# Scores and maxima of an attention layer from stacked keys and queries, in place of row-tiled matmuls

## The chip, the cores and the metric

The kernel runs on one core of a Trainium2 chip. The metric is the time of the whole kernel on the device in microseconds, lower is better. Engines are named TensorE (PE; PEld is its weight load), VectorE (DVE), ScalarE (ACT), GpSimd (POOL) and SyncE (SP, which here only issues DMAs).

## The reference

The input x is 4 batches of 1024 tokens of 512 features, float32. Three layers follow one another, each on the normalised x and each added to it: a feed-forward layer with ternary weights (half its result is added), an attention layer, and the same feed-forward layer again.

```python
x = x + 0.5 * ffn(layernorm(x))
kqv = layernorm(x) @ Wqkv + bqkv                      # 16 heads of 32
scores = einsum('bsnh,btnh->bnst', k, q) / sqrt(32)   # k: rows, q: columns
scores = triu(scores) - 10000 * tril(ones, k=-1)
attn = softmax(scores, axis=2)
x = x + einsum('bnkq,bknh->bqnh', attn, v) @ Wo + bo
x = x + 0.5 * ffn(layernorm(x))
```

A matmul of the attention layer gets float32 accuracy from three faster ones: each operand is held as a high part and the rest (HI and LO), and HI·HI, LO·HI and HI·LO are summed in the bank.

## The kernel before

The work is cut into slots. Each batch has 40 of them, ten rows for each of 4 groups of 4 heads; 21 slots come before (the head) and 10 after (the tail). Every engine walks through the same slots in order, and what a slot holds is written out by hand in tables of rows (GROUP0_ROWS and so on, from L86): `P` is a projection of keys or queries (12 matmuls of 128x512 at L1173), `A` a block of maxima, `M`, `N` and `C` the rows of the maxima, the rows of the inverses and the end of a chunk, `V` the values, `O` the output projection, `T1` to `T3` transposes of normalised tiles, `F1` and `F2` the feed-forward products, `X` loads of x, `LV` and `LO` loads of weights, `W` the preparation of a weight. Ahead of its uses each slot has one step of scores, and the values of the step before it.

A step of scores (`scores`, L1253) works on 4 heads, each in a bank of its own. The 32 rows of keys and queries of a head lie on partitions 32h to 32h+31, so that the matmuls of the four heads use different rows of the array: three terms of four matmuls of 32 rows (L1266), then four of 2 rows (L1274) that add minus the maximum of each query, from `mneg`. ScalarE exponentiates the four banks into `prob` (L1099), GpSimd masks the diagonal ones (L808), and the next slot's TensorE multiplies them with the values (L1294, 128 rows to 32 columns, float32).

The maxima come from a second pass over the scores, in the other orientation: block `A` (L1232) makes 3 terms of four 32-row matmuls into four banks. VectorE masks each bank, writes it to `masked_scores` and keeps its maximum (`maximum`, L900); ScalarE takes the exponentials of that with their sum (`block_sums`, L1065), the first three heads in the slot of the block and the fourth in the next slot, after that slot's exponentials. TensorE transposes the maxima of a chunk (`M`), ScalarE and VectorE split them into `mrow`, and SP copies them to `mneg` (`rows`, L660). Seven banks are a ring in order of use; the eighth gathers the values.

A projection is split by ScalarE (high half with the bias, `high`, L1019) and VectorE (low half, `low`, L881), straight into `kT` and `qT`, where scores and maxima read it. Per group there are four: keys and queries of chunk 0 and of chunk 1. SP's queue is in the order of the slots (L692 and behind): stores, kept weights, loads, rows of the maxima and inverses, and the weights of the next group behind the second pair of projections (`load_qk`, L649).

```python
for term, (x, y) in enumerate(((HI, HI), (LO, HI), (HI, LO))):
    for kb, off, at in parts:
        for h in range(4):
            row = slice(HD * h, HD * h + HD)
            nc.tensor.matmul(psum(u, h)[:, at:at + CW - off],
                             kT[g % 2][row, x, P * kb:P * kb + P], query_piece(b, g, c)[row, y, off:CW], ...)
```

Of the kernel before, what the change touches and what calls it, by code (L numbers as in the profile page):

```python
# [5 lines left out]
F32 = mybir.dt.float32  # L6
# [6 lines left out]
P = 128  # L13
# [5 lines left out]
CW = 512  # L19
# [55 lines left out]
def pieces(b, g):  # L75
    second = (Q_, K_) if g == 0 else (K_, Q_)
    return [("P", b, g, K_, 0), ("P", b, g, Q_, 0)] + [("P", b, g, j, 1) for j in second]
# [9 lines left out]
    "C P | A | LO",  # L87
# [7 lines left out]
    "T3.2 F2.1 | A | X3.5",  # L95
    "F2.2 P | A",
)
GROUP1_ROWS = (
    "C T3.3 P | A | X3.6",
# [7 lines left out]
    "T3.6 F2.5 | A | LV X1.1",  # L107
# [3 lines left out]
    "C T1.0 F2.7 P | A | X1.3",  # L111
# [5 lines left out]
    "M T1.6 F1.5 | A",  # L117
    "T2.2 T1.7 F1.6 | A",
    "T2.3 F1.7 | A",
    "T2.4 P | A",  # L120
)
GROUP3_ROWS = (
    "C T2.5 P | A",
    "N M T2.6 V.0 | A",
    "T2.7 V.1 | A",
    "C P | A",
    "P | A",
    "N V.2 | A",
    "M V.3 V.4 | A",
    "V.5 | A",  # L130
    "V.6 V.7 | A",
    "P | A",
# [3 lines left out]
    "V.4 | A | X1.0",  # L136
    "N M V.5 | A | X1.1 | W",
# [6 lines left out]
    "F1.1 | A",  # L144
# [3 lines left out]
    "C F1.2 P | A",  # L148
# [7 lines left out]
    "F1.5 | A",  # L156
# [3 lines left out]
    "C P | A",  # L160
# [7 lines left out]
    "T2.6 T2.7 | A",  # L168
    "P | A",
)  # L170
FIRST_GROUP3_ROWS = (
    "C P | A",
    "N M V.0 | A",
    "V.1 | A",
    "C P | A",
    "P | A",
    "N V.2 | A",
    "M V.3 V.4 | A",
    "V.5 | A",
    "V.6 V.7 | A",  # L180
    "P | A",
# [3 lines left out]
    "C P | A | LO",  # L185
# [7 lines left out]
    "F2.1 | A",  # L193
# [3 lines left out]
    "C P | A | X3.5",  # L197
    "N M T3.2 P | A",
# [6 lines left out]
    "T3.5 O.7 | A",  # L205
# [3 lines left out]
    "C P | A",  # L209
# [54 lines left out]
    "P | A | | W",  # L264
# [88 lines left out]
for s in SLOTS:  # L353
    small = [u not in PRODUCTS for u in s.uses()]
    assert small == sorted(small, reverse=True)
SETUP_USES = 6
# [11 lines left out]
class Banks:  # L368


    def __init__(self):
# [12 lines left out]
        def use(u):  # L384
            nonlocal full, freed
            take(u, 4 if u[0] == "A" else 1)
            if u != BIAS:
                full += 1
                self.full[u] = full
# [16 lines left out]
def macaron_kernel(nc, x, wqkv, bqkv, wo, bo, wf, bf, out):  # L406
    with ExitStack() as ctx:
# [24 lines left out]
        ones = sb("ones", [P, P])  # L432
        onesr = sb("onesr", [P, P], F32R)
        pick = sb("pick", [8, P], F32R)
# [14 lines left out]
        mrow = sb("mrow", [4 * QPC, 2, 2, P], F32R)  # L449
        rrow = sb("rrow", [4 * QPC, 2, P], F32R)  # L450
# [7 lines left out]
        hi_done = sem("hi_done")  # L458
# [877 lines left out]
```

## Time and profile before

| | |
|---|---|
| median of 3 runs | 1118.87 us (1113.22, 1118.87, 1119.31) |
| profiled execution: own time, span | 1115.44 us, 1113.7 us |
| mean granted clock of TensorE | 0.983 of full speed |
| TensorE busy, matmuls | 1067.9 us (96%), 9472 |
| ScalarE, VectorE, GpSimd busy | 921.7 (83%), 738.9 (66%), 344.0 us (31%) |
| DMA | 77.71 MB, 20.5% of 16 engines on the SP queue |

The span is the time between the first and the last instruction of the profiled execution; its own time has the start and the end around it. Matmuls overlap, so their mean duration is longer than the distance from one to the next: what a use of TensorE costs is read from the start of its first matmul to the start of the next use.

### The profile page before, as it was taken

The page shows a single profiled execution, that of the slowest core. Times are in us where ns is not written, and L with a number is a line of the kernel's source. Part 1 is how long each engine was busy: PE and PEld are TensorE (multiplying, and loading weights), DVE is VectorE, ACT ScalarE, POOL GpSimd, SP SyncE. Part 2 cuts the span into 40 slices and gives each one's busy share as a digit, 9 for nine tenths or more (in the row PEclk, how much of TensorE's full clock was granted, in tenths as well). Part 3 has the DMA queues.
Part 4 walks back from the last instruction along what each step waited for, and adds up shares of the span by engine and source line. Part 5 has one row for each costly group of instructions (what it writes and reads, how often), then busy time and mean ns, then how long its engine had stood idle before and what let it go on. Part 6 is the DMA issues. An engine that isn't in the chain of part 4 may idle for free.

```text
span 1113.7 us, 26124 instructions
## 1 busy us (share of the span) xinstructions
PE 1067.9 (96%) x9472; PEld 691.1 (62%) x9472; DVE 738.9 (66%) x2306; ACT 921.7 (83%) x2577; POOL 344.0 (31%) x471
## 2 busy tenths in 40 slices
PE   5799999999999999999999999999999999999896
PEld 3576656565666565665666666675666666665465
DVE  6866577787535767789644766789744667765344
ACT  2269998999989989889988988878988998999641
POOL 3841232233001313345201322435401322311343
PEclk8898999999999999999999999999999999998999
DMA  6463211021004110421112211421112212000121
GB/s 207 153 217 125 97 50 40 3 78 50 24 19 154 32 59 31 158 73 43 38 41 87 77 59 50 144 78 40 51 40 86 69 40 69 21 12 13 60 66 38
DMA packets 42015, 77.71 MB, mean 70 GB/s; under 512 B 5536, under 2 KB 11680, under 8 KB 41888
## 3 DMA queue, kind: packets, MB, share of 16 engines
q1 hardware_dynamic: 41888, 76.04, 20.5%
q8 instruction: 76, 1.25, 0.5%
q14 instruction: 51, 0.42, 0.1%
HBM read 49.81 MB, written 25.17 MB: 67 GB/s over the span
## 4 chain that ended last, share of the span: by engine, by line
PE 76%; ACT 11%; DVE 6%; issue 2%; POOL 2%; DMA 1%; SPq 0%; DVEq 0%; ACTq 0%; POOLq 0%
PE bank L1173 31%; PE bank L1294 10%; PE bank L1232 10%; PE bank L1266 10%; PE bank L1195 7%; ACT masked_scores L1073 6%; ACT prob L1099 4%; PE bank L1184 3%; PE bank L1274 3%; DVE masked_scores L909 2%; DVE st L859 1%; DMA xt<-in_L_attn_x_dram 1%; DVE hn L878 1%; POOL xt L769 1%; PE bank L1251 1%
## 5 line engine op out<-in xcount | busy, mean ns | idle before, releaser
L909 DVE CUSTOM_DVE_ANT_0 masked_scores<-bank,mask 128x512 f32<-128x512 f32 (+3 forms) x768 | 379.6, 554 | 221.3 <-PE bank L1232 220.2
L1073 ACT ACTIVATE masked_scores<-masked_scores,mst 128x512 f32<-128x512 f32 (+3 forms) x768 | 467.7, 620 | 2.9 <-DVE mst L909 2.9
L1099 ACT ACTIVATE prob<-bank 128x512 f32<-128x512 f32 (+1 forms) x640 | 302.0, 559 | 58.5 <-PE bank L1274 57.4
L1173 PE MATMUL bank<-hT,wqk 128*128 128x512 f32 x768 | 190.9, 397 | 0.0
L808 POOL TENSOR_SCALAR_AFFINE_SELECT prob<-prob 128x512 f32<-128x512 f32 (+1 forms) x96 | 78.6, 819 | 346.5 <-ACT prob L1099 345.8
L1266 PE MATMUL bank<-qT,kT 32*128 32x512 f32 (+2 forms) x2304 | 169.6, 378 | 4.5 <-DVE kT L886 1.6
L1232 PEld LDWEIGHTS bank<-kT,qT 32*128 32x128 f32 x2304 | 94.4, 185 | 115.6 <-issue 52.8
L1232 PE MATMUL bank<-kT,qT 32*128 32x512 f32 (+2 forms) x2304 | 161.2, 377 | 3.4 <-ACT prob L1099 2.6
L1173 PEld LDWEIGHTS bank<-hT,wqk 128*128 128x128 f32 x768 | 140.4, 188 | 37.9 <-ACT prob L1099 8.2
L1073 ACT ACTIVATION_READ_ACCUMULATOR masked_scores<-masked_scores,mst 128x1 f32 x768 | 156.4, 204 | 0.0
L1266 PEld LDWEIGHTS bank<-qT,kT 32*128 32x128 f32 x2304 | 97.7, 185 | 70.4 <-issue 48.4
L1195 PE MATMUL bank<-wfT,hts 128*128 128x512 f32 x512 | 138.3, 414 | 1.5 <-DVE hts L884 1.5
L1294 PE MATMUL bank<-prob,v 128*32 128x512 f32 (+3 forms) x1344 | 138.7, 500 | 0.0
L1195 PEld LDWEIGHTS bank<-wfT,hts 128*128 128x128 f32 x512 | 94.4, 194 | 24.5 <-ACT prob L1099 2.6
L769 POOL TENSOR_TENSOR xt<-xt,hb 128x512 f32<-128x512 f32 x64 | 82.3, 1286 | 77.0 <-DVE hn L878 77.0
L1173 PE MATMUL bank<-wvo,hts 128*128 128x512 f32 x384 | 97.2, 403 | 5.0 <-POOL hts L776 5.0
L1173 PE MATMUL bank<-wvo,hT 128*128 128x512 f32 x384 | 96.1, 402 | 1.2 <-DVE qT L886 1.2
L1173 PEld LDWEIGHTS bank<-wvo,hts 128*128 128x128 f32 x384 | 70.7, 190 | 24.4 <-ACT prob L1099 6.0
L1173 PEld LDWEIGHTS bank<-wvo,hT 128*128 128x128 f32 x384 | 71.3, 191 | 19.5 <-ACT prob L1099 2.7
L1184 PE MATMUL bank<-ident,hn 128*128 128x128 f32 x384 | 59.7, 284 | 13.5 <-DVE hn L878 13.5
L1274 PE MATMUL bank<-mneg,onesr 2*128 2x512 f32 (+2 forms) x768 | 69.9, 350 | 2.1 <-DMA mneg<-mrow 2.1
L859 DVE BATCH_NORM_STATS2 st<-xt 128x6 f32<-128x512 f32 x96 | 65.9, 686 | 5.2 <-DMA xt<-in_L_attn_x_dram 3.2
(87 smaller groups left out, 971.7 us busy)
## 6 DMA issues: line engine op xcount, KB each, us to landing
wqk<-weight_scratch SPq DMA_DIRECT2D x30, 512.0 KB, 3.4
wvo<-weight_scratch SPq DMA_DIRECT2D x20, 512.0 KB, 6.0
xt<-in_L_attn_x_dram SPq DMA_DIRECT2D x32, 256.0 KB, 4.2
residual_scratch<-xt SPq DMA_DIRECT2D x32, 256.0 KB, 2.0
xt<-residual_scratch SPq DMA_DIRECT2D x32, 256.0 KB, 3.1
out_dram<-xt SPq DMA_DIRECT2D x32, 256.0 KB, 2.0
o<-in_L_attn_Wqkv_dram SPq DMA_DIRECT2D x12, 256.0 KB, 4.7
weight_scratch<-o SPq DMA_DIRECT2D x6, 512.0 KB, 3.0
```

The lines of the kernel that those rows point to most:

```text
L769: nc.gpsimd.tensor_tensor(to, to, (bo2 if l == 1 else hb)[:, :], ALU.add).then_inc(xb_done[l], 1)
L808: nc.gpsimd.affine_select(out=part, in_=part, compare_op=ALU.is_ge, fill=0.0, base=0, pattern=[[0, 4], [0, m], [1, P]], channel_multiplier ...
L909: nc.vector.tensor_tensor_reduce(masked_scores[:, h, at:at + n], psum(u, h)[:, at:at + n], mask[:, off:off + n], -SCALE, BIG, ALU.add, ALU ...
L1073: nc.scalar.activation(of, of, ACT.Exp, bias=mst[:, c + kc, to:to + 1], scale=-1.0, accum_out=ssum[:, c + kc, to:to + 1]).then_inc(a_free, 1)
L1099: nc.scalar.activation(prob[:, at % 2, h, off:CW], psum(("S", b, n), h)[:, off:CW], ACT.Exp, scale=SCALE)\
L1173: m = nc.tensor.matmul(psum(u), left(x, k), right(y, k), start=(n == 0), stop=(n == len(terms) - 1))
L1184: m = nc.tensor.transpose(psum(u)[:, P * k:P * k + P], hn[:, TURN[u] % 2, P * k:P * k + P], ident[:, :])
L1195: m = nc.tensor.matmul(psum(u), h[:, part, k, :], wfT[:, k, :], start=(k == 0 and part == HI), stop=(k == KC - 1 and part == LO))
L1232: m = nc.tensor.matmul(psum(u, h)[:, at:at + n], query_piece(b, g, c)[row, x, P * r:P * r + P], kT[g % 2][row, y, CW * kc:CW * kc + n], st ...
L1266: nc.tensor.matmul(psum(u, h)[:, at:at + CW - off], kT[g % 2][row, x, P * kb:P * kb + P], query_piece(b, g, c)[row, y, off:CW], start=(ter ...
L1274: m = nc.tensor.matmul(psum(u, h)[:, at:at + CW - off], onesr[row, :], mneg[row, c, off:CW], start=False, stop=(kb == keys[-1]))
L1294: m = nc.tensor.matmul(accv[HD * h:HD * h + HD, off:CW], v_of(b, g, kb, h), prob[:, at % 2, h, of:of + CW - off], start=(kb == 0), stop=(k ...
```

## The change

Keys and queries of a projection are now stacked. `kst` holds for each head, on partitions 0 to 95, the keys' parts HI, LO, HI, and on 96 and 97 ones; `qst` holds HI, HI, LO of the queries, and on 96 and 97 the high and low part of minus the maximum. One matmul a head over 98 rows gives the scores, one over 96 rows the block of maxima. To bring the four heads of a projection, which come out on 128 partitions, onto 32 partitions side by side, the columns of the weights are reordered so that head h of feature q is on partition 4q + h; the projection is split into one tile, `stage`, and three DMAs of 256 KB from it build a stack (`stack`, on SP, in the slots that MOVES gives). ScalarE waits with the next high half until the last stack has landed. Each head of scores and maxima has its own bank wait and its own signal.

Beside that: three stacks each of keys and queries; `prob` is a ring of 6 heads (8 before), `masked_scores` 2 (4 before), `mrow` one buffer (2 before); ScalarE's order is exponentials of heads 0 and 1, the fourth sum of the last block, exponentials of heads 2 and 3; the mask of a diagonal step is cut in two where the ring ends; and the rows are rearranged: projections stand in rows 8, 9, 1 and 2 of a group (8, 9, 2 and 4 for group 0 of a batch that follows, before 9, 0, 1, 2 or 9, 0, 3, 4), and none in row 0.

```diff
 def pieces(b, g):
-    second = (Q_, K_) if g == 0 else (K_, Q_)
-    return [("P", b, g, K_, 0), ("P", b, g, Q_, 0)] + [("P", b, g, j, 1) for j in second]
+    return [("P", b, g, K_, 0), ("P", b, g, Q_, 0), ("P", b, g, Q_, 1), ("P", b, g, K_, 1)]
...
 GROUP0_ROWS = (
-    "C P | A | LO",
+    "C | A | LO",
     "N M P | A | X3.0",
     "P | A | X3.1",
...
-    "T3.2 F2.1 | A | X3.5",
-    "F2.2 P | A",
+    "F2.1 P | A | X3.5",
+    "T3.2 P | A",
...
+NPIECE, NPROB = 3, 6
+STACK, ROWS = 3 * HD, 3 * HD + 2
...
+MOVES = [[] for _ in SLOTS]
+for at, s in enumerate(SLOTS):
+    for u in s.uses():
+        if u[0] == "P":
+            old = outlived(u)
+            MOVES[at + 1 if old is None else max(at + 1, SLOT_OF[old])].append(u)
...
-        kT = [sb(f"kT{n}", [P, 2, S], F32R) for n in range(2)]
-        qT = sb("qT", [P, 3, 2, CW], F32R)
-        mneg = sb("mneg", [P, CHUNKS, CW], F32R)
-        prob = sb("prob", [P, 2, 4, CW])
+
+        kst = [sb(f"kst{n}", [P, 4, CW], F32R) for n in range(NPIECE)]
+        qst = [sb(f"qst{n}", [P, 4, CW], F32R) for n in range(NPIECE)]
+        stage = sb("stage", [P, 2, CW], F32R)
+        prob = sb("prob", [P, NPROB, CW])
...
-        masked_scores = sb("masked_scores", [P, 4, CW])
-        rall = sb("rall", [8, CW], F32R)
+        masked_scores = sb("masked_scores", [P, 2, CW])
...
+        def heads_inside(w, of):
+
+            return of.rearrange("p (k h q) -> p k q h", k=KC, h=4) if w[0] == "QK" else of
...
+            def stack(u):
+
+                sp.wait_ge(ring_free, freed(u))
+                if outlived(u) is not None:
+                    sp.wait_ge(s_full, 4 * outlived(u) + 4)
+                n, _ = piece(u)
+                to, parts = (kst[n], (HI, LO, HI)) if u[3] == K_ else (qst[n], (HI, HI, LO))
+                for j, part in enumerate(parts):
+                    sp.dma_start(to[HD * j:HD * j + HD, :, :].bitcast(F32), stage[:, part, :].bitcast(F32))\
+                        .then_inc((kst_in if u[3] == K_ else qst_in)[n], 16)
...
+            for n in range(NPIECE):
+                nc.gpsimd.memset(kst[n][STACK:ROWS, :, :].bitcast(F32), 1.0).then_inc(set_pool, 1)
...
                 for h in range(4):
-                    if EARLIER[u] is not None:
-                        dve.wait_ge(a_free, block_at(EARLIER[u], h))
+                    dve.wait_ge(ring_full, full(u) - 3 + h)
+                    if h >= 2:
+                        dve.wait_ge(a_free, block_at(u, h - 2))
+                    elif EARLIER[u] is not None:
+                        dve.wait_ge(a_free, block_at(EARLIER[u], h + 2))
...
                 if kind == "P":
...
+                    at = PROJECTIONS.index(u)
+                    if at:
+                        act.wait_ge(*stacked(PROJECTIONS[at - 1]))
+                    i = nc.scalar.activation(stage[:, HI, :], psum(u), ACT.Identity, bias=bias_of(u[3], u[2]))
...
-                    exponentials(b, s.step)
+                    exponentials(b, s.step, (0, 1))
                 if k and SLOTS[k - 1].blocks:
                     block_sums(SLOTS[k - 1].blocks[-1], (3,))
+                if s.step is not None:
+                    exponentials(b, s.step, (2, 3))
...
                 elif kind == "A":
                     _, b, g, c, kc, _ = u
...
+                    pe.wait_ge(*stacked(("P", b, g, Q_, c)))
+                    pe.wait_ge(*stacked(("P", b, g, K_, kc)))
+                    for h in range(4):
+                        bank_free(u, h)
                         for j, r, at, keys, _ in block_tiles(u):
                             n = max(HALF, keys)
...
+                            m = nc.tensor.matmul(psum(u, h)[:, at:at + n], queries_of(b, g, c)[0:STACK, h, P * r:P * r + P],
+                                                 keys_of(b, g, kc)[0:STACK, h, 0:n], start=(j == 0), stop=(j == len(u[5]) - 1))
+                        m.then_inc(ring_full, 1)
...
                 if keys[0] == 0:
                     pe.wait_ge(mrow_in[c], 32 * group(b, g))
...
+                for h in range(4):
+                    bank_free(u, h)
+                    for kb, off, at in parts:
+                        key = P * (kb % QPC)
+                        m = nc.tensor.matmul(psum(u, h)[:, at:at + CW - off], keys_of(b, g, kb // QPC)[0:ROWS, h, key:key + P],
+                                             queries_of(b, g, c)[0:ROWS, h, off:CW], start=(kb == keys[0]), stop=(kb == keys[-1]))
+                    m.then_inc(s_full, 1)
```

## Rows read from the trace of the kernel before

**Rows 1.** The page: busy time by engine, and the chain that ended last.
```profile
PE 1067.9 (96%) x9472; PEld 691.1 (62%) x9472; DVE 738.9 (66%) x2306; ACT 921.7 (83%) x2577; POOL 344.0 (31%) x471
...
PE 76%; ACT 11%; DVE 6%; issue 2%; POOL 2%; DMA 1%; SPq 0%; DVEq 0%; ACTq 0%; POOLq 0%
...
PE bank L1173 31%; PE bank L1294 10%; PE bank L1232 10%; PE bank L1266 10%; PE bank L1195 7%; ACT masked_scores L1073 6%; ACT prob L1099 4%; PE bank L1184 3%; PE bank L1274 3%; DVE masked_scores L909 2%; DVE st L859 1%; DMA xt<-in_L_attn_x_dram 1%; DVE hn L878 1%; POOL xt L769 1%; PE bank L1251 1%
```

**Rows 2.** Busy time in stretches: PE, PEld, DVE, ACT, POOL (instructions), clock, DMA share, GB/s.
```profile
500.00:525.00 25.00, 23.80 (x212) 14.43 (x210) 24.42 (x71) 21.83 (x56) 13.80 (x20) 1.00 0.13 44
...
550.00:575.00 25.00, 25.00 (x209) 15.41 (x208) 13.09 (x41) 23.21 (x60) 0.00 (x0) 1.00 0.13 44
...
66.00:72.00 6.00, 6.00 (x50) 4.76 (x49) 4.04 (x19) 3.24 (x10) 4.45 (x4) 1.00 0.93 290
```

**Rows 3.** Timeline of TensorE, batch 2: start us, length us, instructions merged.
```profile
612.04 3.04 PE L1173 MATMUL bank<-hT,wqk 128*128 128x512 f32 x12
...
615.01 0.97 PE L1266 MATMUL bank<-qT,kT 32*128 32x512 f32 x12
...
615.80 0.42 PE L1274 MATMUL bank<-mneg,onesr 2*128 2x512 f32 x4
...
616.15 0.86 PE L1294 MATMUL bank<-prob,v 128*32 128x256 f32 x16
...
621.01 0.98 PE L1266 MATMUL bank<-qT,kT 32*128 32x512 f32 x12
...
622.16 1.07 PE L1294 MATMUL bank<-prob,v 128*32 128x512 f32 x8
...
623.15 0.97 PE L1232 MATMUL bank<-kT,qT 32*128 32x512 f32 x12
...
624.05 1.20 PE L1173 MATMUL bank<-wvo,hts 128*128 128x512 f32 x4
```

**Rows 4.** Timeline of TensorE where full-size products meet other uses.
```profile
586.17 5.73 PE L1173 MATMUL bank<-wvo,hT 128*128 128x512 f32 x24
...
1063.82 2.09 PE L1195 MATMUL bank<-wfT,hts 128*128 128x512 f32 x8
...
1065.75 2.89 PE L1173 MATMUL bank<-wvo,hts 128*128 128x512 f32 x12
...
1075.24 2.09 PE L1195 MATMUL bank<-wfT,hts 128*128 128x512 f32 x8
...
1077.27 0.86 PE L1294 MATMUL bank<-prob,vx 128*32 128x256 f32 x16
```

**Rows 5.** Timeline of the SP queue in row 2 of a group.
```profile
610.41 1.12 SPq L664 DMA_DIRECT2D mneg<-mrow  x2
...
611.63 0.38 SPq L657 DMA_DIRECT2D wqk<-weight_scratch  x1
```

**Rows 6.** Timeline of ScalarE and of VectorE around the same row.
```profile
608.79 0.19 ACT L1073 ACTIVATION_READ_ACCUMULATOR masked_scores<-masked_scores,mst 128x1 f32 x1
...
615.44 0.69 ACT L1025 ACTIVATE qT<-bank,bqk 128x512 fp32r<-128x512 f32 x1
...
608.85 0.27 DVE L886 SCALAR_TENSOR_TENSOR mrow<-bank,mrow 16x128 fp32r<-16x128 f32 x1
...
616.16 0.75 DVE L886 SCALAR_TENSOR_TENSOR qT<-bank,bqk,qT 128x512 fp32r<-128x512 f32 x1 [1.99 <-ACT qT L1025]
```

**Rows 7.** The page: DMA issues, KB of each and median us to landing.
```profile
wqk<-weight_scratch SPq DMA_DIRECT2D x30, 512.0 KB, 3.4
...
residual_scratch<-xt SPq DMA_DIRECT2D x32, 256.0 KB, 2.0
```

**Rows 8.** Timelines of TensorE and ScalarE in the head.
```profile
60.72 3.02 PE L1173 MATMUL bank<-hT,wqk 128*128 128x512 f32 x12
...
68.28 0.98 PE L1232 MATMUL bank<-kT,qT 32*128 32x256 f32 x24
...
63.77 0.69 ACT L1025 ACTIVATE qT<-bank,bqk 128x512 fp32r<-128x512 f32 x1 [1.52 <-PE bank L1173]
```

More of the change, by code:

```diff
@@ L155 @@
     "T1.5 | A",
-    "F1.5 | A",
+    "F1.5 P | A",
     "P | A",
@@ L196 @@
 LAST_GROUP1_ROWS = (
-    "C P | A | X3.5",
-    "N M T3.2 P | A",
+    "C T3.2 | A | X3.5",
+    "N M P | A",
     "F2.2 P | A | X3.6",
@@ L355, with piece, outlived @@
     assert small == sorted(small, reverse=True)
+PROJECTIONS = [u for u in USES if u[0] == "P"]
+NPIECE, NPROB = 3, 6
+STACK, ROWS = 3 * HD, 3 * HD + 2
+def piece(u):
+    n = 2 * (u[1] * GROUPS + u[2]) + u[4]
+    return n % NPIECE, n // NPIECE + 1
+def outlived(u):
+    n = 2 * (u[1] * GROUPS + u[2]) + u[4] - NPIECE
+    if n < 0:
+        return None
+    last = (6, 9) if u[3] == K_ else (2, 9)
+    return n // 2 * STEPS + last[n % 2]
+SLOT_OF = {s.b * NSTEP + s.step: k for k, s in enumerate(SLOTS) if s.step is not None}
+MOVES = [[] for _ in SLOTS]
[4 more added lines that the diff above has]
+            MOVES[at + 1 if old is None else max(at + 1, SLOT_OF[old])].append(u)
+assert [u for moves in MOVES for u in moves] == PROJECTIONS
 SETUP_USES = 6
@@ L387, in use @@
             if u != BIAS:
-                full += 1
+                full += 4 if u[0] == "A" else 1
                 self.full[u] = full
@@ L458, in macaron_kernel @@
         hi_done = sem("hi_done")
+        kst_in, qst_in = ([sem(f"kst_in{n}") for n in range(NPIECE)], [sem(f"qst_in{n}") for n in range(NPIECE)])
         s_full, s_exp = sem("s_full"), sem("s_exp")
@@ L549, in before, with keys_of, queries_of, stacked @@
             return (b, g - 1) if g else (b - 1, GROUPS - 1)
-        def query_piece(b, g, c):
-            return qT[:, (group(b, g) * CHUNKS + c) % 3, :, :]
+        def keys_of(b, g, kc):
+            return kst[piece(("P", b, g, K_, kc))[0]]
+        def queries_of(b, g, c):
+            return qst[piece(("P", b, g, Q_, c))[0]]
+        def stacked(u):
+            n, times = piece(u)
+            return (kst_in if u[3] == K_ else qst_in)[n], 48 * times
+        def place(n, h):
+            return (4 * n + h) % NPROB
+        def head_runs(n):
+            m = min(4, NPROB - place(n, 0))
+            return [(0, m)] + ([(m, 4 - m)] if m < 4 else [])
         def chunk(b, n):
@@ L707, in _ @@
                         store(u)
+                for u in MOVES[k]:
+                    stack(u)
                 for n in SLOTS[k - 1].weights if k else []:
@@ L1093, in high_output, with exponentials @@
                 i.then_inc(o_hi, 1)
-            def exponentials(b, n):
+            def exponentials(b, n, heads):
                 off = live(n % STEPS)
                 at = step(b, n)
-                for h in range(4):
-                    nc.scalar.activation(prob[:, at % 2, h, off:CW], psum(("S", b, n), h)[:, off:CW], ACT.Exp, scale=SCALE)\
+                for h in heads:
+                    act.wait_ge(s_full, 4 * at + h + 1)
+                    if 4 * at + h >= NPROB:
+                        act.wait_ge(value_done, (4 * at + h - NPROB) // 4 + 1)
+                    nc.scalar.activation(prob[:, place(at, h), off:CW], psum(("S", b, n), h)[:, off:CW], ACT.Exp, scale=SCALE)\
                         .then_inc(s_exp, 1)
```

172 lines of the change are left out of this document (74 added, 98 removed).

## The prediction

> **What bounds the kernel now.** Read the page first: TensorE is busy 96% of the span, ScalarE 83%, VectorE 66%, and the chain that ended last lies on TensorE for 76% [rows 1]. Its costliest members are the twelve-matmul products of L1173 (31%); scores (L1266 and L1274, 13%) and maxima (L1232, 10%) come next. So the question is what TensorE pays for scores and maxima. Then the busy time by stretch: between 550 and 575 us TensorE has no gap and ScalarE has 1.8 us left of 25; between 500 and 525, where transposes are dense, VectorE is the fullest at 24.4 and TensorE is short by 1.2 [rows 2]. Whatever ScalarE is made to wait for has little room. Then TensorE's timeline, a slot at a time: from 615.01 to 621.01, 6.0 us [rows 3]. Last, the SP queue and ScalarE in row 2 of a group, since the change puts a transfer between two of ScalarE's steps there.
>
> **Scores and maxima on TensorE.** A full block of scores now costs 1.14 us (615.01 to 616.15): three rounds of four concurrent 32-row matmuls to 615.80, then one round of 2-row ones. A full block of maxima costs 0.90 (623.15 to 624.05): three rounds [rows 3]. The change makes each four matmuls, one a head, with 98 or 96 rows. Their price is that of a product's matmul: 24 take 5.73 us and 12 take 3.04, so each further one takes (5.73 - 3.04)/12 = 0.224, call it 0.227, in the middle of the reading [rows 3, 4]. Four make 0.91. What lies between two uses: eight matmuls (1.82) and the next full-size product starts at 1.93, a gap of 0.11; before values it is 2.03, a gap of 0.21 [rows 4]; twelve (2.72) before scores as they are now take 612.04 to 615.01, 2.97, a gap of about 0.22 once a late wait of 0.03 is taken off [rows 3].
> So scores become 0.91 + 0.21 = 1.12, less by 0.02. Maxima become 0.91 + 0.11 = 1.02, more by 0.12: they lose a round, since three terms that ran four heads at a time become four full-width streams. The step from a product to scores falls from 0.22 to 0.11, less by 0.11. Values keep their 0.99 [rows 3]. Net: -0.01 a slot, over 160 slots **-2 us**. 3840 of the 9472 matmuls go, but hardly any streaming time. Both ends: if full-size uses follow each other with no gap, each slot saves another 0.22 (-37 us in all); if every head's matmul, which now has its own bank wait before it, pays the 0.11, six more a slot are +0.66, or +106 us. I take the value in between, since waits that are already met don't show inside the products.
> The Trainium skill (TensorEngine Tiling (Array Packing), Tiling Modes) says that a change of tiling mode drains TensorE. The change takes two of four such changes out of a slot; by that rule alone scores and maxima should be a gain, and the sum would be that of the first rival below. The rows agree that a change costs something (0.21 against 0.11), but it is small beside the lost round.
>
> **The stack.** Each of the 64 projections now goes to one staging tile, and three transfers of 256 KB copy it. ScalarE may not write the next projection's high half before the last stack has landed. Landing: one store of 256 KB takes 2.0 us from issue, one load of 512 KB 3.4 [rows 7]; at 290 GB/s, the most that a stretch shows at a DMA share of 0.93 [rows 2], 768 KB take 2.7 us, and with about 1.1 of fixed time 3.8. Bounds: 2.0, if the three run side by side, and 10.2, three times the 512 KB load. I take 3.8.
> - Rows 1 and 2 of a group hold the second pair. In row 2 SP is busy with the rows of the maxima until 611.53 and then with a weights' load [rows 5]. These wait for the low half of the maxima's rows, which VectorE begins at 608.85, right behind its last maximum. With two score buffers instead of four that maximum waits for ScalarE's sum of the second head, whose read now begins at 608.79 [rows 6]; a maximum is then still to be made, so all of this comes about 0.7 us later. The stack is thus issued at about 612.8 and, behind the 512 KB load, lands near 617.5. ScalarE wants the stage at 615.44 [rows 6]: a stall of about 2 us, and behind ScalarE stand the next exponentials, behind VectorE's low half the bank that the next maxima need. TensorE is ahead by part of it; I take 1.2 us for each of the 12 groups that have this pair: **+14**. Bounds 0 and 3 us each, 0 to 36.
> - Rows 8 and 9 hold the first pair. No other rows are queued on SP, the stack is issued about 2.2 us after the slot begins and lands at 6.0, when ScalarE wants it (0.4 us after TensorE ends a slot of about 6 us, as at 615.44): 0.2 for 15 groups, **+3**.
> - The first maxima of the next group are in row 1 and wait for the query stack of row 9, a full chain later: 0.7 high half, 0.75 low half [rows 6], 3.8 landing. With a full row 0 in between this is covered; where row 0 holds almost nothing (four groups) TensorE waits 1.5: **+6**.
> - In the head the second projection begins at 60.72, as the first ends, the maxima begin at 68.28 and ScalarE takes the query's high half at 63.77 [rows 8]; the DMA engines are 93% busy from 66 to 72 [rows 2]. Two stacks in a chain, each after a high and a low half and slowed to about 5 us (62 to 67, then 68.5 to 74), move the first maxima from 68.3 to about 74; two later pairs add some: **+9**, between 3 and 20.
>
> **The other edits.** Two score buffers: in rows with two transposes VectorE waits inside the maxima for sums that ScalarE does after two high halves; where VectorE is the last [rows 2], it is ahead of nothing and loses about 0.3 in some ten slots, **+3**. Semaphores by head: exponentials can begin after one matmul instead of sixteen, maxima after one instead of twelve, some 0.6 to 0.8 us earlier; where TensorE bounds, that is only latency, where it stood short of full it gives back some, **-6**. The ring of six for the exponentials, the split of the mask, the single row buffer, five small loads of biases, strided splits of the weights and three memsets of two rows: nothing each, hidden under the next slot's work or under the wait for the first weights; if that cover is gone, 0.3 to 2 us each. The wait for the maxima's rows moves ahead of all scores of steps 0 and 3: the rows' transfer ends well before, except in the last batch.
>
> **The sum.** The profiled execution took 1115.44 us, for a span of 1113.7, and stands 3.4 under the median of 1118.87. 1115.4 - 2 + 14 + 3 + 6 + 9 + 3 - 6 = **1142.4 us**, some 2% over either. What a measurement of this kernel can tell from no change is about 0.5%.
>
> **Rivals.**
> First, *faster*: the gaps between full-size uses vanish and the stacks land in 2 to 3 us, so only the head's cost and a part of the others is left: 1115 - 37 - 6 + 9 + 8 = 1089. For it speaks that the projections keep their slots' distance; against it, SP's two pairs of row transfers in front of the stack [rows 5]. 0.19.
> Second, *no change*: as forecast, but ScalarE's stalls are taken up by its slack of 1.8 us in 25 [rows 2] and the head's by idle engines: within 1113 to 1124. 0.13.
> Third, *much slower*: TensorE can't load a head's weights past that head's own bank wait. Place: every head of scores and maxima; price: 0.11 each, six more a slot, full or half: 1142 + 53 to 106, 1195 to 1248. It decides as soon as waits are met only just in time, which the two-buffer scheme makes likelier; against it, the sixteen matmuls of scores have four such waits now and show none of it. 0.16.
> The Trainium skill (TensorE: Matmul & The Clock Gate, Part 3) has it that each semaphore increment at a matmul's end is written one after another, 26.3 ns each; an estimate by that page for six more increments a slot is 25 us, which would make the sum 1167, in the same direction. No row here shows increments so close together.
>
> **How the numbers follow.** The forecast has 0.52, the rivals 0.19, 0.13 and 0.16. The range 1098 to 1188 holds the forecast with its bounds, the second rival and the upper part of the first; it leaves out the third and the fastest of the first. Faster by over 0.5%: 0.19; within: 0.13; slower: 0.68.
>
> **What would show it.** In the changed profile: 768 matmuls each for scores and maxima at a spacing near 0.227; from first maximum to next use 1.02; ScalarE's high halves of projections waiting for the stack's DMA, longest in row 2 of a group, some 1 to 2 us; TensorE's longest new wait at the first maxima in the head. The forecast is wrong if ScalarE never waits there, if a slot without projection falls below 5.8 us where it is 6.0 now, or if idle time shows between the heads' matmuls.

## The result, and the profile after

The changed kernel takes 1367.5 us (median of 4 runs, 1362.9 to 1372.3), the kernel before in the same runs 1116.2 (4 runs, 1113.2 to 1119.3): a ratio of 1.225, with a 95% interval of 1.219 to 1.231. It is slower by 251 us where 26 were forecast, and far outside the range of 1098 to 1188. One run in all is left out of the ratios: one of the four of **tiny** below, 1667.4 us at a granted clock of 0.56.

The page of the changed kernel: the lines that answer to [rows 1] and [rows 7], and the three groups of instructions that matter. Behind the bar of a group stand its busy time, the mean ns of one instruction, and the idle time before them with what ended most of it:

```profile
span 1365.8 us, 19813 instructions
...
PE 1152.2 (84%) x5632; PEld 776.5 (57%) x5632; DVE 762.6 (56%) x2306; ACT 949.7 (70%) x2577; POOL 356.1 (26%) x505
...
PE 46%; DMA 24%; ACT 9%; DVE 9%; SPq 6%; issue 3%; POOL 2%; DVEq 0%; ACTq 0%; POOLq 0%
...
L989 DVE CUSTOM_DVE_ANT_0 masked_scores<-bank,mask 128x512 f32<-128x512 f32 (+3 forms) x768 | 408.2, 556 | 329.9 <-ACT masked_scores L1153 225.4
...
L1310 PE MATMUL bank<-kst,qst 96*128 96x512 f32 (+2 forms) x768 | 220.2, 408 | 156.8 <-DVE stage L964 103.7
...
L1103 ACT ACTIVATE stage<-bank,bqk 128x512 fp32r<-128x512 f32 x64 | 43.9, 687 | 185.3 <-DMA qst<-stage 74.4
...
kst<-stage SPq DMA_DIRECT2D x96, 256.0 KB, 5.6
qst<-stage SPq DMA_DIRECT2D x96, 256.0 KB, 5.9
wqk<-weight_scratch SPq DMA_DIRECT2D x30, 512.0 KB, 4.7
```

DMA now holds 24% of the chain that ended last, where it held 1% [rows 1]. TensorE's idle time is 1365.8 - 1152.2 = 213.6 us against 1113.7 - 1067.9 = 45.8 before: 168 more. The other 84 of the 252 us are in its busy time, 1152.2 against 1067.9, though the changed slots take no longer when they run undisturbed (below): the granted clock averages 0.893 instead of 0.983. Behind the first 20 us of the trace, every idle stretch of TensorE of over 2.5 us lies in microseconds at a granted clock of 0.50, the lower of its two levels (1.2 GHz), or is followed by them; TensorE is busy for 233 us at that clock, where it was for 35 before.

Two new waits stand out. ScalarE's high halves of projections (L1103) waited 185 us, 148 of them for the stacks' DMA (the waits give 74.4 in 13 times for `qst` and 73.2 in 16 for `kst`), and VectorE's maxima (L989) waited 225 us for ScalarE's sums. The timelines of the four engines around row 2 of a group (start us, length us; row 2 begins at 449.05, row 3 at 454.48) show how the first reaches TensorE. In brackets stands how long the engine sat idle before, and what ended that:

```profile
451.38 1.98 SPq L736 DMA_DIRECT2D qst<-stage  x3
...
459.92 0.69 ACT L1103 ACTIVATE stage<-bank,bqk 128x512 fp32r<-128x512 f32 x1 [5.02 <-DMA qst<-stage]
...
460.64 0.75 DVE L964 SCALAR_TENSOR_TENSOR stage<-bank,bqk,stage 128x512 fp32r<-128x512 f32 x1 [5.89 <-ACT stage L1103]
...
456.29 0.73 PE L1310 MATMUL bank<-kst,qst 96*128 96x512 f32 x2
461.44 0.92 PE L1310 MATMUL bank<-kst,qst 96*128 96x512 f32 x2 [4.42 <-DVE stage L964]
462.30 0.79 PE L1328 MATMUL bank<-rows_of,pick 8*128 8x512 f32 x1
463.02 5.49 PE L1255 MATMUL bank<-wvo,hts 128*128 128x512 f32 x12
468.31 1.24 PE L1343 MATMUL bank<-qst,kst 98*128 98x512 f32 x4
```

The stack is issued from 451.38 and ScalarE goes on at 459.92, 8.5 us later. VectorE's low half stands behind ScalarE, and behind VectorE the bank of the third head of the maxima: TensorE stops for 4.42 us, and its next twelve matmuls then take 468.31 - 463.02 = 5.3 us, for which [rows 3] have 3.0. Row 3 lasts 13.8 us; in the kernel before the same row of the same group took 6.0.

The same happens at the other pair of projections, in rows 8 and 9. The stack of row 8 is issued in row 9 and still on its way when ScalarE wants the stage in row 0 of the next group:

```profile
424.65 1.93 SPq L736 DMA_DIRECT2D kst<-stage  x3
...
432.78 0.69 ACT L1103 ACTIVATE stage<-bank,bqk 128x512 fp32r<-128x512 f32 x1 [4.51 <-DMA kst<-stage]
...
434.31 1.07 PE L1310 MATMUL bank<-kst,qst 96*128 96x512 f32 x2 [3.45 <-DVE stage L964]
```

Over the whole trace ScalarE's wait for the stage costs TensorE 56 us in 12 rows 3 and 43 us in 14 rows 0; the maxima's own wait for a query stack adds 20.5 us in 12 rows 1 and 17.6 in the head.

The stack before that of row 2 is issued from 434.28. The busy time in stretches from then on (columns as in [rows 2]: length; PE, PEld, DVE, ACT and POOL busy; clock, DMA share, GB/s):

```profile
438.00:440.00 2.00, 1.55 (x8) 0.00 (x0) 1.93 (x9) 1.92 (x5) 0.00 (x0) 0.50 1.04 124
440.00:442.00 2.00, 0.00 (x0) 0.00 (x0) 0.01 (x1) 1.23 (x5) 0.68 (x1) 0.50 1.05 132
442.00:444.00 2.00, 1.63 (x7) 1.63 (x8) 0.80 (x7) 0.00 (x0) 0.00 (x0) 0.50 1.06 389
```

The DMA engines are full in all three, but bring 124 to 132 GB/s while the stack is copied and 389 when the four loads of `wvo` behind it run. That became the theory to test: **A, landing**, a transfer that writes 32 partitions is slow. Against it stood **B, structure**: the two score buffers, the single stage and the moved rows. Measured over the 64 stacks in the trace's landing records, from the first issue to the last packet of the third transfer, a stack takes a median of 8.1 us (7.8 to 9.8).

### The profile page after: what moved, and what is told of

It is laid out like the page before. It is cut to its first block, busy times and chain, and to the rows that moved or that the text cites. A ratio compares the mean times of both kernels' runs of the same rounds, so it can differ in the third digit from the quotient of the medians.

```text
span 1365.8 us, 19813 instructions
## 1 busy us (share of the span) xinstructions
PE 1152.2 (84%) x5632; PEld 776.5 (57%) x5632; DVE 762.6 (56%) x2306; ACT 949.7 (70%) x2577; POOL 356.1 (26%) x505
## 4 chain that ended last, share of the span: by engine, by line
PE 46%; DMA 24%; ACT 9%; DVE 9%; SPq 6%; issue 3%; POOL 2%; DVEq 0%; ACTq 0%; POOLq 0%
PE bank L1255 18%; DMA qst<-stage 15%; PE bank L1310 9%; DMA kst<-stage 8%; PE bank L1363 5%; PE bank L1277 5%; PE bank L1343 5%; SPq L736 4%; ACT masked_scores L1153 4%; DVE stage L964 3%; ACT stage L1103 2%; PE bank L1266 2%; DVE masked_scores L989 2%; ACT prob L1182 1%; SPq L745 1%
## 5 line engine op out<-in xcount | busy, mean ns | idle before, releaser
L989 DVE CUSTOM_DVE_ANT_0 masked_scores<-bank,mask 128x512 f32<-128x512 f32 (+3 forms) x768 | 408.2, 556 | 329.9 <-ACT masked_scores L1153 225.4
L1310 PE MATMUL bank<-kst,qst 96*128 96x512 f32 (+2 forms) x768 | 220.2, 408 | 156.8 <-DVE stage L964 103.7
L1182 ACT ACTIVATE prob<-bank 128x512 f32<-128x512 f32 (+1 forms) x640 | 318.6, 553 | 37.6 <-PE bank L1343 29.7
L1310 PEld LDWEIGHTS bank<-kst,qst 96*128 96x128 f32 x768 | 127.0, 207 | 295.4 <-DVE stage L964 115.9
L1343 PE MATMUL bank<-qst,kst 98*128 98x512 f32 (+2 forms) x768 | 189.9, 370 | 14.3 <-DVE mst L989 8.8
L885 POOL TENSOR_SCALAR_AFFINE_SELECT prob<-prob 128x512 f32<-128x512 f32 (+2 forms) x128 | 83.7, 658 | 423.0 <-ACT prob L1182 422.8
L1103 ACT ACTIVATE stage<-bank,bqk 128x512 fp32r<-128x512 f32 x64 | 43.9, 687 | 185.3 <-DMA qst<-stage 74.4
L1343 PEld LDWEIGHTS bank<-qst,kst 98*128 98x128 f32 x768 | 136.5, 199 | 52.9 <-DVE mst L989 20.8
L1277 PE MATMUL bank<-wfT,hts 128*128 128x512 f32 x512 | 153.2, 448 | 5.1 <-DVE hts L962 2.1
L964 DVE SCALAR_TENSOR_TENSOR stage<-bank,bqk,stage 128x512 fp32r<-128x512 f32 x64 | 48.0, 750 | 194.1 <-ACT stage L1103 194.1
```

The lines of the kernel that those rows point to most:

```text
L885: i = nc.gpsimd.affine_select(out=part, in_=part, compare_op=ALU.is_ge, fill=0.0, base=0, pattern=[[0, heads], [0, m], [1, P]], channel_mu ...
L964: i = nc.vector.scalar_tensor_tensor(dst, src, first[0], hi.bitcast(F32), first[1], ALU.subtract)
L989: nc.vector.tensor_tensor_reduce(masked_scores[:, h % 2, at:at + n], psum(u, h)[:, at:at + n], mask[:, off:off + n], -SCALE, BIG, ALU.add, ...
L1182: nc.scalar.activation(prob[:, place(at, h), off:CW], psum(("S", b, n), h)[:, off:CW], ACT.Exp, scale=SCALE)\
L1277: m = nc.tensor.matmul(psum(u), h[:, part, k, :], wfT[:, k, :], start=(k == 0 and part == HI), stop=(k == KC - 1 and part == LO))
L1310: m = nc.tensor.matmul(psum(u, h)[:, at:at + n], queries_of(b, g, c)[0:STACK, h, P * r:P * r + P], keys_of(b, g, kc)[0:STACK, h, 0:n], sta ...
```

## The experiments

Each run is compared with the kernel before on the same chip (1117 to 1118 us there). The diffs show the deciding lines, shortened and without bitcasts. In **tiny**, **spread**, **one** and the runs that leave stacks unfilled, the stacks are filled with ones at the start, and SP waits for that before its first slot.

### How much is the landing

**tiny**: each transfer of a stack brings 16 of 512 columns; all waits stay. The scores and maxima are computed mostly from the ones.

```diff
-    sp.dma_start(to[HD * j:HD * j + HD, :, :], stage[:, part, :])
+    sp.dma_start(to[HD * j:HD * j + HD, :, 0:16], stage[:, part, 0:16])
```

> Each of the three transfers of a stack copies 16 of the 512 columns, so 8 KB in place of 256 KB; waits, order and TensorE's work stay (the stacks hold mostly ones, so the output is another; both sets of stacks are filled once at the start). Theory A, the landing: the 252 us lost come from the time in which 768 KB land (8.5 us from the first issue in row 2 of a group, where ScalarE and then TensorE wait), and from the clock behind these waits. Then the time falls to 1105 to 1150, the granted clock is back at 0.97 or more, and ScalarE no longer waits for a stack by more than 10 us in all. Theory B, the structure: the waits come from the single stage, the two score buffers and the ring of banks by head, whatever the transfer carries. Then it stays above 1250, and idle time before the maxima stays above 80 us.

Measured: 1180.3 us, ratio 1.055 (1.053 to 1.058); a stack is complete after 3.1 us, the clock is at 0.965. 187 of the 251 us go with the bytes, so A carries most of it, and B, which allowed nothing below 1250, falls as the whole cause. But 62 us are left, more than A allowed, and ScalarE still waits 12.7 us for stacks where A had 10.

**spread**: all bytes, each transfer to 128 partitions of 2 KB in place of 32 of 8 KB. Scores and maxima are again not the reference's.

```diff
-    sp.dma_start(to[HD * j:HD * j + HD, :, :], stage[:, part, :])
+    sp.dma_start(to[:, j, :], stage[:, part, :])
```

> The same three transfers with all their 768 KB, but each writes one tile of 128 partitions by 2 KB in place of 32 partitions by four times 2 KB (values of the stacks are wrong so, which costs no time). Theory A1, the shape: the landing is slow because each transfer writes only 32 partitions (from 436 to 442 us the sixteen engines were full at 124 to 132 GB/s, and at 316 to 389 GB/s in the loads behind). Then a transfer lands in 3 to 4 us in place of 5.7, ScalarE's stall in row 2 shrinks to 0 to 2 us, and the time is 1130 to 1200. Theory A2, the bytes: 768 KB from SBUF to SBUF are slow in any shape; then landing and time stay within 2% of the changed kernel's 1367.

Measured: 1211.0 us, ratio 1.083 (1.081 to 1.086), 11 above the range of A1, which had nothing for the structure; A2 falls. The page's landings:

```profile
kst<-stage SPq DMA_DIRECT2D x96, 256.0 KB, 2.5
qst<-stage SPq DMA_DIRECT2D x96, 256.0 KB, 2.8
```

A transfer lands in 2.5 to 2.8 us instead of 5.6 to 5.9, a whole stack in 3.8 instead of 8.1. The same bytes, issued and waited for at the same places, cost 157 us less by their shape alone. ScalarE's waits for the stage in rows 3 fall from 69.6 to 29.4 us, those in rows 0 from 60 to nearly nothing.

**one**: only the first of the three transfers, and only it waited for; two thirds of a stack are left out.

```diff
-    for j, part in enumerate(parts):
+    for j, part in list(enumerate(parts))[:1]:
```

> Only the first of the three transfers is made, 256 KB to 32 partitions, and its 16 are waited for (two thirds of each stack keep ones). By A1, 256 KB at 130 GB/s take 2.0 us and some 2 us of fixed time: landing 4 us after the issue, 1130 to 1190. By theory B 1250 or more. If the cost goes by the number of bytes it should lie at a third of the way from the kernel with small transfers to the changed one, if it goes by a threshold (what ScalarE can be made to wait before TensorE feels it) nearer to the former.

Measured: 1218.0 us in a single run, above A1's range as well. A single transfer to 32 partitions is there after 4.0 us, and it costs about what three to 128 partitions cost in 3.8. The times follow when the stack is complete, not its bytes: 3.1, 3.8, 4.0 and 8.1 us go with 1180, 1211, 1218 and 1367, and 24, 768, 256 and 768 KB.

**traffic32**: the kernel before, with three copies of 256 KB to 32 partitions behind each projection that only later copies wait for.

```diff
+    for j in range(3):
+        sp.dma_start(scr[HD * j:HD * j + HD, :, :], hb[:, :]).then_inc(scr_in, 16)
```

> The kernel before, with the stack's traffic added and nobody waiting for it but the queue itself: behind each projection three transfers of 256 KB from one tile of 128 partitions to 32 partitions of a spare tile. If the traffic itself costs (loads and rows that it delays), the time is 1140 to 1200; if the cost is only in the waits for it, 1115 to 1125.

Measured: 1149.0 us, ratio 1.027 (1.025 to 1.029). The copies land in 5.9 us at the median, three of them in 8.1, with no stack in sight; the 512 KB loads of `wqk` land in 7.0 instead of 3.4 [rows 7]. Of the 31 us, 25 lie in six waits of TensorE for transfers that stood behind copies on the queue (five for the rows of the maxima, 16.0 us, one for a load of `wqk`, 9.3); the kernel before has one of these, 2.1 us. In the changed kernel TensorE waits once for rows of the maxima, 3.0 us, and never for such a load. So these 31 us are a cost of their own in this order of the queue and no part that can be taken off the 251: there, what A costs is the waiting for the stacks.

### Which partitions make a transfer slow

**shapes**: the kernel before, with two such copies behind each projection, in four shapes that take turns.

```diff
+    kind = (at + at // 4) % 4
+    for j in range(2):
+        if kind == 0:   sp.dma_start(scr[HD * j:HD * j + HD, 0:4, :], hb[:, :])      # L679
+        elif kind == 1: sp.dma_start(scr[0:64, 2 * j:2 * j + 2, :], hb[:, :])        # L681
+        elif kind == 2: sp.dma_start(scr[32:96, 2 * j:2 * j + 2, :], hb[:, :])       # L683
+        else:           sp.dma_start(scr[:, j, :], hb[:, :])                         # L685
```

> The kernel before, with two copies of 256 KB behind each projection that nobody but the next copies wait for, in four shapes that take turns: to 32 partitions x 8 KB, to partitions 0-63 x 4 KB, to partitions 32-95 x 4 KB, to 128 partitions x 2 KB. It is read by the landing of each shape and the DMA rate of its stretches. Theory A1 (the time is set by how many partitions are written): 32 partitions about 5.7 us as in the stacks, 64 about half way (4), both placements alike, 128 about 2.5. Theory A3 (the Trainium skill, SBUF - State Buffer, Door 1: partitions 0-31 and 32-63 share their ports, 64-95 have others): 0-63 lands as 32 does (about 5.7), 32-95 as 128 does (about 2.5 to 3). Theory A4 (a copy inside the core is slow in any shape): all four about 5.7; spread has already spoken against it. Whole time 1122 to 1150.

The view of each of the four lines (issue time ns, then the landings):

```profile
L679 SPq DMA_DIRECT2D scr<-hb x32: 594/604/1493, 63.9 to 985.4; - x32
...
DMA to landing us min/median/max: 4.2/5.4/7.9
...
L681 SPq DMA_DIRECT2D scr<-hb x32: 553/596/1027, 70.5 to 992.0; - x32
...
DMA to landing us min/median/max: 4.2/5.3/6.7
...
L683 SPq DMA_DIRECT2D scr<-hb x32: 571/603/624, 80.7 to 998.0; - x32
...
DMA to landing us min/median/max: 2.9/3.4/8.8
...
L685 SPq DMA_DIRECT2D scr<-hb x32: 497/560/603, 86.1 to 979.1; - x32
...
DMA to landing us min/median/max: 2.3/2.5/4.1
```

The two copies of a projection are issued one behind the other, so these are times under that load (the single copy of **one** took 4.0). 64 partitions from 0 on land hardly sooner (5.3) than 32 do (5.4), where A1 had 4; 64 from 32 on land in 3.4, 128 in 2.5. The two shapes of 64 differ in nothing but their place: it is not how many partitions, but which. The Trainium skill (SBUF — State Buffer, Door 1: The DMA port swizzle) says that partitions p and p + 32 share a port and that p + 64 has another, so that 0 to 63 reach no more ports than 0 to 31, half of all. The trace agrees that 0 to 63 gain next to nothing over 32. Two things differ. By the page 32 to 95 reach every port as 0 to 127 do, and A3 had them at 2.5 to 3; they need 3.4, for which no run gives the reason. And the rate falls further than the page's half, to 124 to 132 GB/s in the changed kernel where the loads have 384 to 389. The whole kernel takes 1117.3 us in a single run, against 1118.3: two copies that nothing waits for, mostly in faster shapes, cost nothing here.

**twoq**: the kernel after, complete, with the third transfer of a stack (to partitions 64 to 95) issued by GpSimd.

```diff
+    for u in MOVES[k]:        # GpSimd, ahead of its other work in a slot
+        pool.wait_ge(ring_free, freed(u)); pool.wait_ge(s_full, 4 * outlived(u) + 4)
+        pool.dma_start(to[HD * 2:HD * 3, :, :], stage[:, part, :]).then_inc(kst3_in[n] or qst3_in[n], 16)
```

> The kernel after with the third transfer of each stack (to partitions 64-95, whose ports are others than those of 0-63 by the rows of shapes) issued by GpSimd from its own queue while SP issues the first two; nothing is left out. Theory Q1 (two queues run side by side, so the stack is complete some 2 us earlier): 1280 to 1330 against 1367. Theory Q2 (the same engines serve both queues in turn; the Trainium skill, SBUF - State Buffer, Can I just issue two DMAs to hit both halves?, says they serialize): 1350 to 1390, the last part of a stack landing 8 us or more after the first issue as now.

Measured: 1367.9 us, ratio 1.224 (1.220 to 1.228), as the kernel after. The page's landings:

```profile
kst<-stage SPq DMA_DIRECT2D x64, 256.0 KB, 6.3
qst<-stage SPq DMA_DIRECT2D x64, 256.0 KB, 7.2
...
kst<-stage POOLq DMA_DIRECT2D x32, 256.0 KB, 6.1
qst<-stage POOLq DMA_DIRECT2D x32, 256.0 KB, 6.6
```

GpSimd issues its transfer 0.3 us after SP's first at the median, so they do run together. Each gets slower, and the stack is complete after 8.1 us as before. A second queue is no way out; this was Q2.

### What the structure costs

**before_ms2**: the kernel before with two score buffers, nothing else.

```diff
-    if EARLIER[u] is not None: dve.wait_ge(a_free, block_at(EARLIER[u], h))
+    if h >= 2: dve.wait_ge(a_free, block_at(u, h - 2))
+    elif EARLIER[u] is not None: dve.wait_ge(a_free, block_at(EARLIER[u], h + 2))
-    masked_scores[:, h, ...]
+    masked_scores[:, h % 2, ...]      # at both places, and the tile is [P, 2, CW]
```

> The kernel before, with two score buffers in place of four and the waits that go with it, nothing else. Theory B1 (the rest of the cost, 62 us with the stacks' bytes all but gone, comes from the coupling of VectorE's third maximum to ScalarE's first sum): 1150 to 1180. Theory B2 (it comes from the order of the rows, the projections moved) and theory B3 (it comes from the one stage, each projection waiting for the copy of the last, or from the heads' own waits): 1117 to 1125.

Measured: 1184.3 us, ratio 1.058 (1.054 to 1.063): 66 us for one small edit, which the prediction had at 3. The timelines of VectorE and ScalarE in one slot:

```profile
494.23 0.69 DVE L911 CUSTOM_DVE_ANT_0 masked_scores<-bank,mask 128x512 f32<-128x512 f32 x1 [0.56 <-PE bank L1234]
...
495.22 0.69 DVE L911 CUSTOM_DVE_ANT_0 masked_scores<-bank,mask 128x512 f32<-128x512 f32 x1 [0.29 <-ACT masked_scores L1075]
...
496.89 0.69 DVE L911 CUSTOM_DVE_ANT_0 masked_scores<-bank,mask 128x512 f32<-128x512 f32 x1 [0.98 <-ACT masked_scores L1075]
...
492.53 2.06 ACT L1101 ACTIVATE prob<-bank 128x512 f32<-128x512 f32 x4 [0.47 <-PE bank L1276]
494.45 0.64 ACT L1075 ACTIVATE masked_scores<-masked_scores,mst 128x384 f32<-128x384 f32 x1
...
495.05 0.62 ACT L1065 ACTIVATE o<-bank 128x512 f32<-128x512 f32 x1
495.53 0.63 ACT L1041 ACTIVATE hts<-bank 128x512 fp32r<-128x512 f32 x1
496.01 0.76 ACT L1075 ACTIVATE masked_scores<-masked_scores,mst 128x512 f32<-128x512 f32 x1
```

VectorE's second maximum waits for the last sum of the block before, which ScalarE makes only behind four exponentials (492.53 to 494.45); its third waits for the first sum of this block, which stands behind the copy of the output and a high half (495.05, 495.53). 1.3 us are lost in this slot, and VectorE's later work in it (residuals, low halves) stands behind them. Such waits come 281 times, in 145 slots, 123.2 us in all; before TensorE's scores (L1268) stand 21 us of idle time, 18.6 of them for maxima, against 4.5 in the kernel before. All of TensorE's idle time grows by 25 us, its busy time by 40, 33 of it in the scores' own lines (L1268 and L1276), at a clock of 0.975 against 0.983. That the buffers cost 66 us is shown; what stretches the scores' busy time was not taken apart. Four buffers let VectorE run through all four maxima while ScalarE is still at its exponentials.

**tiny_ms4**: tiny, with the four buffers and the waits of before; one tile of ones stands for the keys.

```diff
-    kst = [sb(f"kst{n}", [P, 4, CW], F32R) for n in range(NPIECE)]
+    kst = [sb("kst", [P, 4, CW], F32R)] * NPIECE     # small key transfers go to kdst
-    masked_scores = sb("masked_scores", [P, 2, CW])
+    masked_scores = sb("masked_scores", [P, 4, CW])
```

> The kernel tiny with four score buffers and the waits of before; the room comes from one tile of ones that stands for all three key stacks, whose small transfers go to a tile of their own. Theory B1 (two buffers): 1120 to 1145, and VectorE's wait of 217 us for ScalarE's sums goes. Theories B2 and B3: 1165 to 1185, that wait being only the other face of TensorE's pace.

Measured: 1140.5 us, ratio 1.017 (1.013 to 1.021): 40 of tiny's 62 us are the two buffers (B1). VectorE's wait for ScalarE's sums falls from 217 us to 8.8.

**tiny_rows**: tiny with all the row tables (GROUP0_ROWS to the tail) of before; the order within a quadruple of projections, queries first, stays.

```diff
-    "C | A | LO",
+    "C P | A | LO",
...
```

> The kernel tiny (the three transfers cut to 16 of 512 columns) with the row tables of before, so that projections, transposes and values are in the rows that they had. Theory B2 (order of the rows): 1120 to 1150 against 1180 for tiny. Theories B1 and B3: 1170 to 1200, as the rows with projections and first maxima get closer and the stage waits may even rise.

Measured: 1255.6 us, ratio 1.121 (1.117 to 1.126), 75 us **slower** than tiny. No theory said so. The waits say why:

```profile
PEld bank L1314 <- DMA qst<-stage: 88.0, 19, 6.5
ACT rows_of L1116 <- PE bank L1328: 74.2, 16, 6.5
PE bank L1314 <- DMA qst<-stage: 71.8, 19, 5.5
```

In the old rows the maxima come sooner behind the projection that they read, and even a stack that is complete after 3.1 us is late for them, 19 times by 3.8 us at the mean. (The lines give total us, times and the longest.) The moved rows are no cost of the change but what it needs; B2 falls.

**after_ms4** and **after_2st**: the kernel after with all transfers at full size, and once four score buffers, once two stages. The room comes as in tiny_ms4. In after_2st that puts the copies of every fourth stack (the second keys of a group) on other partitions, partly 64 at a time; those stacks are complete after about 8 us too.

```diff
-    act.wait_ge(*stacked(PROJECTIONS[at - 1]))      # after_2st
+    act.wait_ge(*stacked(PROJECTIONS[at - 2]))      # stages[at % 2] in place of stage
```

> The kernel after with all its transfers at full size and in their slots, but four score buffers and their waits. The room comes from one tile of ones that stands for the keys; the key stacks are copied to one tile that nobody reads. The scores and maxima are thus not those of the reference. Theory B1 with costs that add: 1320 to 1335 (40 us less, as tiny_ms4 against tiny). Theory B1 with costs that hide each other behind the landing: 1345 to 1365.

> The kernel after with two stages in place of one: ScalarE's high half waits for the stack before the last one. The room comes from the keys' tile as in after_ms4, so scores and maxima are not those of the reference. Theory C1 (the landing is paid through the stage: ScalarE waits for it, behind it VectorE's low half and the bank of the next maxima): 1250 to 1310, and ScalarE's wait for the stacks under 40 us instead of 148. Theory C2 (it is paid through the maxima's own wait for the stack that they read): 1340 to 1365.

Measured: 1319.1 us, ratio 1.182 (1.178 to 1.186), for the buffers: 48 us less, so their cost adds to that of the landing and does not hide behind it. And 1238.2, ratio 1.108 (1.105 to 1.110), for the second stage: 129 us less, with a stack still complete only after 8.4 us. The waits of after_2st:

```profile
DVE masked_scores L995 <- ACT masked_scores L1162: 217.5, 209, 5.1
...
PE bank L1319 <- DMA qst<-stage: 70.7, 19, 10.6
...
DVE stage L970 <- ACT stage L1112: 62.4, 56, 2.8
```

TensorE's maxima no longer wait for VectorE's low halves; ScalarE's wait for the stacks is gone. What is left of the landing is the maxima's own wait for the query stack, 70.7 us, 49.9 of them in row 1 (mostly 10 to 14 us long). So the landing was paid mainly through the stage: C1, and 12 us below its range.

**tiny_ms4_2st**: both on tiny.

```diff
     masked_scores = sb("masked_scores", [P, 4, CW])     # as tiny_ms4
+    stages = [sb(f"stage{n}", [P, 2, CW], F32R) for n in range(2)]
```

> The kernel tiny_ms4 (transfers cut to 16 columns, four score buffers) with two stages as well. Theory B3 (what is left over the kernel before, 22 us with some 9 of it in the head, comes from the one stage): 1125 to 1132. Its rival (it comes from the new order of the rows and the half-empty row 0 before a dense row 1): 1137 to 1143.

Measured: 1134.1 us, ratio 1.015 (1.012 to 1.017). With short transfers the single stage costs 6 us, 4 of them in the head: the first scores start at 104.8 us, in tiny_ms4 at 109.1, before at 99.9. The result lies between the two theories' ranges. Of the 17 us that remain over the kernel before, 5 lie so in the head. Behind the head TensorE no longer waits for any query stack (in the head twice, 3.7 us in all), so the rest lies in the rows and their new order; how it divides was not tried.

## Why the prediction was wrong

**The step that failed is the landing of a stack.** It was put at 3.8 us, from 768 KB at 290 GB/s and 1.1 of fixed time; the runs show 8.1. The 290 was the rate of a stretch in the head of the kernel before, which has no copy of this shape; a stack's transfers write 32 partitions, and run at 124 to 132. The store and the load of [rows 7], from which it was bounded, write DRAM or 128 partitions: neither resembles the transfer. How much hung on it shows in spread, which has exactly the 3.8 us that it assumed, and takes 1211. So the miss of 225 us has two parts: 157 for the landing (1367 - 1211) and 69 for the rest (1211 - 1142), most of it the second step that failed, the two score buffers (48 us by after_ms4).

- **The stall of row 2** (+14): place and mechanism were right (ScalarE waits for the stage, the bank of the next maxima comes late). Forecast for each of 12 groups were 2 us for ScalarE and 1.2 for TensorE; measured are 5.8 and 4.7 at the mean, and in the group shown row 3 grows by 7.8. With the landing as assumed (spread) ScalarE waits 2.9 us in ten of them and TensorE 2.2 in nine. The bound of 3 us a group does not follow from the landing's upper bound of 10.2, which did hold 8.1: an upper bound has to be carried through to the terms that hang on it. A second stage takes 129 us away, here and at the next pair.
- **The pair of rows 8 and 9** (+3) failed by the same step and as badly. The stack was to land 6.0 us into the slot, just when ScalarE wants the stage; issued 1.7 us into it, it lands at 9.8. ScalarE waits 60 us in 14 groups and TensorE 43, where 3 were forecast. In spread both waits are nearly gone (TensorE is idle for 3.6 us in all rows 0 together). A term that sits just inside its cover is as open to an error of the landing as one outside.
- **The next group's first maxima** (+6): TensorE waits 20.5 us for the query stack in 12 rows 1.
- **The clock** was no term of the sum. Behind stalls of 3 to 12 us the granted clock is 0.50, and twelve matmuls take 5.3 us instead of 3.0. TensorE's busy time grows by 84 us, a third of the loss; of all its busy time 233 us lie at 0.50, against 35 before.
- **Two score buffers** were priced at 3 us in ten slots. Alone they cost 66 on the kernel before, 40 on tiny, 48 on after. The step looked at rows where VectorE is the last, and at the sums behind two high halves; missed was that the wait comes in most slots (145 in before_ms2), because ScalarE's first sum stands behind its exponentials, copies and high halves, and that VectorE's later work in the slot moves with it.
- **The head** was put at +9, with the first maxima moved from 68.3 to 74. With stacks of 3.1 us (tiny) they begin at 74.2; with 8.1 us they begin at 80.3, and the first scores come at 129.6, 30 us later than before.
- **TensorE's prices** came out as forecast. The timeline of undisturbed slots of the changed kernel, next to [rows 3]:

```profile
714.52 1.09 PE L1343 MATMUL bank<-qst,kst 98*128 98x512 f32 x4
715.54 1.07 PE L1363 MATMUL bank<-prob,vx 128*32 128x512 f32 x8
716.53 1.21 PE L1310 MATMUL bank<-kst,qst 96*128 96x512 f32 x4
717.58 0.27 PE L1319 MATMUL bank<-ident,mst 128*16 128x128 f32 x1
...
720.46 1.09 PE L1343 MATMUL bank<-qst,kst 98*128 98x512 f32 x4
```

  Scores take 1.02 (forecast 1.12), values 0.99, maxima 1.05 (1.02), and a whole slot 5.94 where it was 6.0. The gap ahead of values (1.02 less four times 0.227) is 0.11, not 0.21: a small part of the first rival was true, some 0.1 a slot. Taking row tiling away removed 3840 of 9472 matmuls and left their streaming time. The sign of being wrong that the prediction named, a slot without projection below 5.8 us, is not met by the 5.94.
- **The rivals.** The third, gaps between heads, is false: 1.02 for four heads, each with its own wait and increment. Where idle time does stand between two heads, as in row 3 above, VectorE's late low half ends it. The Trainium skill (TensorE: Matmul & The Clock Gate, Part 3) has 26.3 ns for each increment where tiles run side by side in the array; laid on four heads one behind the other, an estimate from it would be some 0.1 us more. This trace shows none of that. The first fell with the landing, and would have fallen with a short one: at 3.1 us (tiny) the kernel is still at 1180. By the Trainium skill (TensorEngine Tiling (Array Packing), Tiling Modes) a change of tiling mode drains TensorE; where the change took such a step away, the rows show 0.1 us of gain (0.21 or 0.22 to 0.11). The second rested on ScalarE's slack of 1.8 us in 25, which a stall of 5 does not fit into.
- **The semaphores by head** (-6) were not taken apart by themselves.

## What to carry to other kernels

Before a copy inside SBUF is put between two dependent steps, ask which partitions its destination touches, and count the time of the whole group of transfers to the last landing, not of one transfer alone; then carry the upper bound of that time through every wait behind it, and count the slow clock after each stall. A second buffer at the source of such a copy brings back most of its price (129 us here, of the 157 to 187 that a fast copy would). Halving a ring between two engines that work through their own orders is not a small edit: look at what the releasing engine does first in each slot.

## What the runs showed of the hardware

- Of two 256 KB copies inside SBUF issued one behind the other, one lands in 5.4 us at the median on partitions 0 to 31 (or 32 to 63), 5.3 on 0 to 63, 3.4 on 32 to 95 and 2.5 on all 128 (shapes); a single one on 0 to 31 lands in 4.0 (one). While slow ones run in the changed kernel, the DMA engines count as full (1.04 to 1.09) at 124 to 132 GB/s, and at 389 behind them (1.06), so the DMA share does not tell the rate.
- Two queues do not add for such copies: 6.1 to 7.2 us each instead of 5.6 to 5.9, and the stack is complete after 8.1 us either way (twoq).
- Slow copies hold up what is behind them: the 512 KB loads in 7.0 us instead of 3.4 (traffic32).
- Four matmuls of 96 or 98 rows cost 1.02 to 1.05 us with their gap, twelve of 32 rows 0.90 [rows 3].
